# Transformer block in one program: Q and K stacked in two fp32r parts on 32 rows a head instead of six bf16 part products on 64

## The reference, cut to what matters

```python
xn = layernorm(x)
# attention 1: no softmax; causal; weights 1 - tanh^2 of scaled and shifted scores
energy = (where(causal, -10000, q1 @ k1.T * scale) - threshold) / tau
a1 = 1 - tanh(energy)**2;  s = (a1 / (sum(a1) + 1e-6) @ v1) @ Wo.T
# attention 2: plain softmax over all 512 keys, then a mixture of experts
h = rmsnorm(xn);  ctx = softmax(q2 @ k2.T * scale) @ v2;  x1 = xn + ctx @ wo
h2 = rmsnorm(x1); moe = swiglu_shared(h2) + sum over top 2 of 8 experts
out = x + s * silu(x1 + moe)
```

## Time and profile before

| what | us |
|---|---|
| median of 3 runs (1149.69 to 1155.43) | 1154.11 |
| the profiled execution | 1157.05 |
| its span in the trace | 1155.2 |
| first score matmul of row 0 | 76.4 |
| one row of tokens in the middle (from 485.69 to 621.17, L1193 to L1193) | 135.5 |

### The profile page before, as it was taken

How to read it: one execution, slowest core, us unless ns; L and a number is a source line. 1 busy time by engine, 2 the same in 40 slices (tenths; PEclk the granted TensorE clock), 3 DMA queues, 4 the chain that set the end, 5 groups by cost and what they waited for, 6 DMA issues and landing times.

```text
span 1155.2 us, 18598 instructions
## 1 busy us (share of the span) xinstructions
PE 1032.3 (89%) x6912; PEld 471.8 (41%) x6912; DVE 856.3 (74%) x1716; ACT 652.9 (57%) x888; POOL 347.4 (30%) x194
## 2 busy tenths in 40 slices
PE   3459999989999999999999899999999889999998
PEld 1102355324652346423554245522465235542364
DVE  7447687759977597786877589775986869774872
ACT  4027862588326972378624884269723786248831
POOL 6500335103630154303352035400552033520023
PEclk9558999999999999999999999999999999999999
DMA  5540225103441045201251024310342113500020
GB/s 176 117 54 2 49 68 132 34 2 77 109 68 29 3 96 127 38 20 44 64 141 25 11 63 122 69 28 2 96 116 41 30 29 69 148 9 20 1 75 9
DMA packets 71785, 69.65 MB, mean 60 GB/s; under 512 B 8528, under 2 KB 63056, under 8 KB 71568
## 3 DMA queue, kind: packets, MB, share of 16 engines
q1 hardware_dynamic: 68928, 64.41, 24.7%
q10 hardware_dynamic: 2768, 4.06, 1.0%
HBM read 53.37 MB, written 14.81 MB: 59 GB/s over the span
## 4 chain that ended last, share of the span: by engine, by line
PE 56%; DVE 21%; ACT 11%; DMA 4%; issue 3%; SPq 3%; POOL 1%; ACTq 0%; DVEq 0%; POOLq 0%
PE O L1019 9%; PE O L1035 8%; DVE nmax L677 7%; DVE PT L714 7%; ACT PT L554 6%; PE S L1051 6%; PE S L1053 5%; PE S L994 5%; PE S L1052 5%; PE M L963 4%; PE M L960 4%; PE M L946 2%; DVE PT L840 2%; SPq L337 2%; SPq L327 1%
## 5 line engine op out<-in xcount | busy, mean ns | idle before, releaser
L554 ACT ACTIVATE PT<-S 128x1024 f32<-128x1024 f32 (+1 forms) x448 | 420.7, 971 | 117.3 <-PE S L994 115.0
L677 DVE TENSOR_REDUCE nmax<-M 128x1 f32<-128x512 f32 x512 | 330.6, 685 | 119.4 <-PE M L960 80.4
L714 DVE SCALAR_TENSOR_TENSOR PT<-PT 128x768 f32<-128x768 f32 (+1 forms) x192 | 215.6, 1171 | 96.4 <-ACT PT L554 96.0
L1019 PE MATMUL O<-PT,V 128*12 128x256 f32 (+3 forms) x2816 | 242.2, 424 | 0.0
L423 POOL TENSOR_TENSOR split<-split,parts 128x512 f32<-128x512 f32 x32 | 91.0, 2844 | 433.2 <-ACT parts L514 433.2
L438 POOL TENSOR_TENSOR PT<-PT,CB 128x1024 f32<-128x1024 f32 x56 | 133.2, 2385 | 278.0 <-DMA CB<-scrC 158.2
L588 ACT ACTIVATE PT<-S 128x1024 f32<-128x1024 f32 x72 | 73.9, 1027 | 250.7 <-PE S L1053 250.6
L994 PE MATMUL S<-stackQ,stackK 64*128 64x512 bf16 (+3 forms) x1024 | 192.1, 347 | 21.6 <-DMA stackQ<-mTZ 8.4
L1051 PE MATMUL S<-h2hi,wgu_hi 128*128 128x512 f32 x288 | 150.5, 522 | 0.1
L1035 PE MATMUL O<-PT,wdn 128*128 128x512 f32 x288 | 142.7, 595 | 0.0
L960 PE MATMUL M<-KX,stackQ 128*128 128x512 bf16 x256 | 104.3, 409 | 28.5 <-DMA KX<-scrK 21.3
(11 more groups left out here) (189 smaller groups left out, 1042.5 us busy)
## 6 DMA issues: line engine op xcount, KB each, us to landing
CB<-scrC SPq DMA_DIRECT2D x64, 256.0 KB, 5.7
stackQ<-scrQ SPq DMA_DIRECT2D x192, 64.0 KB
stackK<-scrK SPq DMA_DIRECT2D x192, 64.0 KB
scrQ<-parts SPq DMA_DIRECT2D x16, 384.0 KB, 5.0
scrK<-parts SPq DMA_DIRECT2D x16, 384.0 KB, 7.8
KX<-scrK SPq DMA_DIRECT2D x96, 32.0 KB
PT<-in_w_gu ACTq DMA_DIRECT2D x2, 1152.0 KB, 8.0
xin<-in_x SPq DMA_DIRECT2D x8, 256.0 KB, 2.9
```

The source lines that it names most:

```text
L554: a.activation(PT[:, n % SLOTS, 2 * q * w:2 * q * w + 2 * w].rearrange("p (r n) -> p r n", r=2), S[k][:, :].rearrange("p (r n) -> p r n", ...
L677: v.tensor_reduce(nmax[:, h % 2, h // 2, t:t + 1], M[k][:, :], AX.X, ALU.max, negate=True).then_inc(m_read[k], 1)
L714: v.scalar_tensor_tensor(p, p, 1.0, p, ALU.subtract, ALU.mult).then_inc(weighed, 1)
L1019: last = t_.matmul(O[k][32 * q:32 * q + VW, i0:i1], V[:, j, 4 * g + q, :], PT[:, n % SLOTS, w * q + at:w * q + at + i1 - i0], start=(j == ...
```

## The change

`PAIRS` has three products of two parts, (0,0), (0,1) and (1,0), 24 rows a head, and the parts are fp32r in place of bf16. A head takes 32 rows (`SLOT`), the four heads of a group lie above each other, and the row maximum's two parts are rows 24 and 25. `KX` is 128 rows by 4 heads by 2 groups of fp32r. POOL makes the second part in one instruction; the store of a stack is two fp32 parts, its 12 loads are 8 partitions by 4 groups by 512 fp32. The transposes of the maxima take an fp32r identity. The maxima of Y and Z stand directly behind the score pair of a half, those of heads 2 and 3 of a group behind half 0, those of heads 0 and 1 behind half 1.

```diff
-PAIRS = [(0, 0), (0, 1), (0, 2), (1, 0), (1, 1), (2, 0)]
-HP = H // 2
-HALF = 64
+PAIRS = [(0, 0), (0, 1), (1, 0)]
+PARTS = 2
+SLOT = 32
...
-spread(MAX["Y"], {0: 1, 1: 3, 2: 4, 3: 4, 4: 4})
-spread(MAX["Z"], {5: 3, 6: 4, 7: 4, 8: 5})
+spread_beside("Y", {0: (1, 1), 1: (1, 1), 2: (2, 2), 3: (2, 2), 4: (2, 2)})
+spread_beside("Z", {5: (2, 2), 6: (2, 2), 7: (2, 2), 8: (2, 2)})
...
-        parts = [sb(f"parts{i}", [128, 3, L], bf16) for i in range(2)]
-        stack = {n: sb("stack" + n, [128, HP, L], bf16) for n in ("Q2", "K2", "Q1", "K1")}
-        KX = sb("KX", [128, 2, PADDED, L], bf16)
+        parts = [sb(f"parts{i}", [128, PARTS, L], fp32r) for i in range(2)]
+        stack = {n: sb("stack" + n, [128, NG, L], fp32r) for n in ("Q2", "K2", "Q1", "K1")}
+        KX = sb("KX", [128, 4, PADDED, L], fp32r)
...
-                    for r in range(2):
+                    for i in range(4):
                         for c, pair in enumerate(PAIRS):
-                            sp.dma_start(stack[name][HALF * r + HD * c:HALF * r + HD * c + HD, :, :],
-                                         scratch[name][pair[side]].rearrange("(h r d) n -> r d h n", r=2, d=HD)[r])\
+                            sp.dma_start(stack[name][SLOT * i + HD * c:SLOT * i + HD * c + HD, :, :].bitcast(fp32),
+                                         scratch[name][pair[side]].rearrange("(g i d) n -> i d g n", i=4, d=HD)[i])\
...
-                g.tensor_tensor(s[:, :], s[:, :], p[:, 0, :], ALU.subtract).then_inc(pool_step, 1)
-                g.tensor_tensor(p[:, 1, :], s[:, :], ones[:, 0:1].broadcast_to([128, L]), ALU.mult).then_inc(pool_step, 1)
-                g.tensor_tensor(p[:, 2, :], s[:, :], p[:, 1, :], ALU.subtract).then_inc(parts_ready, 1)
+                g.tensor_tensor(parts[i][:, 1, :], split[i][:, :], parts[i][:, 0, :], ALU.subtract).then_inc(parts_ready, 1)
...
-                        rows = slice(HALF * r, HALF * r + HALF)
+                        rows = slice(SLOT * (2 * q + r), SLOT * (2 * q + r) + SLOT)
...
+                    if n < N1:
+                        for q, part in enumerate((names[:u.cut[n]], names[u.cut[n]:])):
+                            scores(it, n, q)
+                            for name in part:
+                                if name[0] == "max":
+                                    work(u, it, name)
+                            if n in v_at and v_at[n] % NT > 0:
+                                with_v(it, v_at[n], q)
+                            elif n in v_at and q == 0:
+                                with_v(it, v_at[n])
+                            for name in part:
+                                if name[0] != "max":
+                                    work(u, it, name)
+                        continue
```

More of the change, by code:

```diff
@@ L51, in width, with blocks, spread, spread_beside @@
     return L if kind == "all" else sum(L - 128 * j for j in js)
-MAX = {run: [("max", 2 * hp + r, t) for hp in range(*pairs) for t in range(NT) for r in range(2)] for run, pairs in RUNS.items()}
+MAX = {run: [] for run in RUNS}
 EXPERT, END = UNITS, UNITS + NE
 PLACES = {n: [] for n in range(END + 1)}
-def spread(work, counts):
-    at = 0
-    for n, count in counts.items():
-        PLACES[n] += work[at:at + count]
-        at += count
-    assert at == len(work)
-spread(MAX["Y"], {0: 1, 1: 3, 2: 4, 3: 4, 4: 4})
-spread(MAX["Z"], {5: 3, 6: 4, 7: 4, 8: 5})
+HALF1 = set()
+def blocks(run, slots):
+    return [("max", 4 * RUNS[run] + i, t) for t in range(NT) for i in slots]
+def spread(run, counts):
+    work = blocks(run, range(4))
+    for n, count in counts.items():
+        PLACES[n] += work[:count]
+        MAX[run] += work[:count]
+        del work[:count]
+    assert not work
+def spread_beside(run, counts):
+    halves = blocks(run, (2, 3)), blocks(run, (0, 1))
+    for n, of_half in counts.items():
+        for half, count in enumerate(of_half):
+            PLACES[n] += halves[half][:count]
+            MAX[run] += halves[half][:count]
+            if half:
+                HALF1.update(halves[half][:count])
+            del halves[half][:count]
+    assert not any(halves)
+spread_beside("Y", {0: (1, 1), 1: (1, 1), 2: (2, 2), 3: (2, 2), 4: (2, 2)})
+spread_beside("Z", {5: (2, 2), 6: (2, 2), 7: (2, 2), 8: (2, 2)})
 PLACES[3].insert(2, "outT")
@@ L105, in __init__ @@
         self.places = {n: [w for w in work if here.get(w, following if w in AHEAD else own)] for n, work in PLACES.items()}
+        self.cut = {n: sum(w not in HALF1 for w in work) if n < N1 else len(work) // 2 for n, work in self.places.items()}
         self.order = [w for n in sorted(self.places) for w in self.places[n]]
@@ L190, in program @@
         ones = sb("ones", [128, 128])
[L191 to L194, removed]
+        identr = sb("identr", [128, 128], fp32r)
+        nmax = sb("nmax", [128, 4, NG, NT])
+        mh = {run: sb("mh" + run, [128, 4 * PARTS * NT], fp32r) for run in RUNS}
+        mT = {run: sb("mT" + run, [4 * PARTS * NT, 128], fp32r) for run in RUNS}
         stats = sb("stats", [128, NT, 6])
@@ L449, in row @@
                 g.tensor_tensor(VS[:, 0, :, :], V1[:, 1, :, 0:HD], VS[:, 1, :, :], ALU.add).then_inc(v_summed, 1)
[L450 to L456, removed]
+                if following:
+                    second_part(u, "Q2")
+                    second_part(u, "K2")
                 for e in range(1, NE - 1):
                     if following and e < 3:
-                        for _step in split_steps(u, ("Q1", "K1")[e - 1], it + 1, True):
-                            pass
+                        second_part(u, ("Q1", "K1")[e - 1])
                     weigh_expert(it, e)
@@ L983, in scores @@
                 key, query = ("K2", "Q2") if n < N1 else ("K1", "Q1")
[L984 removed]
+                at = 0
                 if n >= N1:
@@ L1155, in row @@
                         pe.wait_ge(setup, 2)
-                    for run, (p0, _p1) in RUNS.items():
-                        if n == NT * (p0 // 2) and n:
+                    for run, g in RUNS.items():
+                        if n == NT * g:
                             pe.wait_ge(row_in[run], (it + 1) * 64)
@@ L1187, in row @@
                     work(u, it, "maxT_W")
-                    for q in range(2):
-                        scores(it + 1, 1, q)
-                    for name in ROWS[it + 1].places[0]:
-                        work(ROWS[it + 1], it + 1, name)
+                    second_scores(ROWS[it + 1], it + 1)
                 for t in range(NT):
@@ L1207, in _ @@
             first_scores(0)
-            for q in range(2):
-                scores(0, 1, q)
-            for name in ROWS[0].places[0]:
-                work(ROWS[0], 0, name)
+            second_scores(ROWS[0], 0)
             for it in range(B):
```

111 lines of the change are left out of this document (52 added, 59 removed).

## The result

| | median, us | runs | ratio to before, 95% interval |
|---|---|---|---|
| before | 1154.3 (1149.7 to 1155.4) | 4 | |
| after | 1284.1 (1277.1 to 1293.1) | 4 | 1.114 [1.105, 1.122] |

What follows compares the result with a forecast made beforehand. Bounds: DVE in units 0 to 8, ACT in units 9 to 15, PE in stage 2 and the experts. A row 0 + 0.5 + 0.7 + 0.8 = +2.0, times 8 = +16, start -8: +8, 1162 us; range 1124 to 1194.

Steps and rivals of the forecast that it cites:

- stage 1: Score stage of each row of tokens: no change in units 0 to 8, +0.5 us a row in units 9 to 15.
- units 0 to 8: First half of stage 1, with the maxima of Y and Z: DVE sets the pace, no change, bounds -1.9 and +0.3.
- Units 9 to 15: Second half of stage 1: PE's half units go from 0.87 to 0.97; +0.5 us a row, bounds 0 and +1.4.
- The load: Every score group: the longer fp32r weight load costs PE 0.10 us, bounds 0 and 0.2; pair to product 0.42.
- Stage 2: Per row: loads add 2.9, less a 1.3 wait and 0.9 idle: +0.7 us, bounds -1.3 and +3.5.
- The 1.3 wait: Stage 2, 7 rows: PE's wait for DVE, slowed by POOL's splits, goes with POOL's shorter work: -1.3 us.
- The experts: Expert stretch of each row: slower fp32r maxima and score groups opening twice, +0.8 us, bounds 0 and +1.5.
- Fewer POOL instructions cost nothing here: Experts: POOL's shorter split adds no time, since PE is the bound there.
- The start: Before the first score matmul: earlier stores and larger packets shorten the DMA queue, -8 us, between -3 and -15.
- The loads are not hidden: Against the faster rival: loads hidden at every score group, 0.32 pair to product, 1120 us, chance 0.3.
- They do not queue either: Against the slower rival: neighbouring heads' loads queue, each pair opens 0.2 later, 1214 us, chance 0.12.
- The maxima do run beside the pair: Against the last rival: stage 1 maxima run after the pair, at most +2 a row, 1162 to 1178, chance 0.08.

Runs made afterwards that it cites:

- runs with fillers: Kernel after, with 2, 4 or 8 overwritten bf16 full-array matmuls ahead of each stage 1 score pair: 1261.5 to 1330.5, 1237.1 and 1273.3 us.
- fp32r run with 64 rows: Kernel after, stage 1 scores and maxima of Y and Z contracting over 64 rows at a time, Exp's scale lowered: 1194.2 us (one run).
- the order alone: Kernel before (bf16, 64 rows a head) with only the change's new places of the maxima: 1160.3 us, ratio 1.005.
- run with POOL's part alone: Kernel before with one POOL instruction a tensor making the second bf16 part, third part left out: 1149.9 us, ratio 0.996.
- run with four fillers: Kernel after, with four overwritten bf16 matmuls of 128 x 128 and 128 columns ahead of each stage 1 score pair: 1237.1 us, ratio 1.070.
- run with the start alone: Kernel before with only the maxima rows of X and W sent ahead of K1's loads at the start: 1150.1 us, ratio 0.996.
- run with POOL's late weighing: Kernel before, one POOL instruction a tensor, but three for the following row's Q1 and K1, delaying the second expert's weighing; third part unused: 1140.3 us, ratio 0.985.
- eight fillers: Kernel after, with eight overwritten bf16 matmuls of 128 x 128 and 128 columns ahead of each stage 1 score pair: 1273.3 us, ratio 1.102.

## Why the prediction was wrong, step by step

**The step that failed is stage 1**, "I take no change, bounds -1.9 and +0.3" and "+0.5, bounds 0 and +1.4". Its prices came from rows at clock 1.00, and the sum had no term for what the change does to the clock: the clock was taken as unchanged without a reason. The measured change is +115.2 in 8 rows, 14.4 a row, of which by the runs with fillers and with 64 rows some 11 is the clock and some 3.5 the change itself at full clock (an estimate). The trace of before could have warned: in the earlier trace rows two maxima on `KX` take 1.01 us, where 0.22 + 0.39 = 0.61 would do by the earlier trace rows; the page's clock row has a 5 in its second and third slice; and from 76.4 to 92.9 stage 1 runs at 0.50 with PE at work. That the array's filling is the cause could not be read from it; it has no stretch of 32-row matmuls.

**At full clock units 0 to 8 were mis-sized too.** In the fp32r run with 64 rows, stage 1 is +3.3 against +0.5. Units 9 to 15 are as forecast, half units of 394.72 - 393.74 = 0.98 for 0.97, and from unit 9's first pair to the end 15.3 for 14.4, inside the bounds of 0 and +1.4. The other 2.4 lie in units 0 to 8, where I took DVE's pace to hide the loads and the order to cost nothing; the order alone cost 0.7 there in bf16. In that run the maxima do not run beside the pair, so how much of the rest holds for the change itself stays open. The bound of -1.9 does not come out of its own terms either: 22.3 - 23.9 is -1.6, and DVE's idle time is 2.2.

```profile
393.74 0.50 PE L997 MATMUL S<-stackQ,stackK 64*128 64x512 f32 x2
394.17 0.62 PE L1022 MATMUL O<-PT,V 128*12 128x256 f32 x8
394.72 0.50 PE L997 MATMUL S<-stackQ,stackK 64*128 64x512 f32 x2
```

**The load was right.** 0.42 from pair to product was forecast, 0.43 measured at full clock; PE's busy time in stage 2 grew by 37.57 - 34.87 = 2.70, forecast 2.9.

**Stage 2 was right**, +0.4 or +0.5 in six of the 8 rows for +0.7 forecast (+0.9 as a mean, with the half clock in the fourth row and +1.9 in the last). The 1.3 wait of the transposes of OS for DVE is gone, as a run with POOL's part alone confirms: -1.5.

**The experts** took +1.0 to +1.5 in the first seven rows for +0.8 forecast, inside the bounds of 0 and +1.5, but not for the reasons given alone. "Fewer POOL instructions cost nothing here" was wrong: the run with POOL's part alone is 0.8 to 1.3 longer there.

**The start** was right in its direction, -11.0 for -8, though that is one profile against one: in the run with four fillers, which is the same up to there, `KX` landed at 40.9, 4.6 later than here. The queue did stop being last: `KX` landed at 36.3 instead of 42.25, the rows of X went out at 54.75, and the first score stands directly behind the transpose of W.

```profile
54.75 2.74 SPq L356 DMA_DIRECT2D stackQ<-mTX  x4
```

```profile
65.13 0.31 PE L972 MATMUL M<-identr,mhW 128*32 128x128 f32 x1 [1.28 <-DVE mhW L690]
65.38 0.80 PE L997 MATMUL S<-stackQ,stackK 32*128 32x512 f32 x4
```

**The rivals.** The loads are not hidden (0.43). They do not queue either (0.5 and more was its mark). The maxima do run beside the pair. None of the rivals named the clock; the slower one's 1214 came nearest to the time by a mechanism that is not there.

## What to carry to other kernels

A change that narrows what matmuls fill of the array is to be priced twice, once at each level of the clock, before anything else is counted; read the granted clock of every stretch of the kernel before and ask which stretches the change makes like the slow ones. When a wait is removed, follow the engine that is now early: POOL's second expert, weighed sooner, took back most of what POOL's shorter split had won.

## What the runs showed of the hardware

- The granted clock fell from 1.00 to 0.50, and stayed there with PE busy 47.01 of 47.80 us, in matmuls on 32 rows of fp32r (stage 1 of the kernel after); in bf16 on 32 rows it did the same (33.33 of 34.20). In stage 1 of rows 2 to 8 it stayed at 1.00 with 64 rows of fp32r, and with four matmuls of 128 x 128 added to each pair. What brings it back 3 us before the end of stage 1 no run isolates.
- Pairs on 64 rows do not keep 1.00 always: in bf16 they ran from 76.4 to 92.9 at 0.50 at the start of the kernel before, and two of the runs with them have one short fall in a stage 1 (from 513.50 in the run with the start alone, from 510.57 in the run with POOL's late weighing).
- Stage 2 after also has 32-row pairs and keeps 1.00 in most rows; there masks and projections of 128 rows stand between them. That this is why was not tested. In the runs with 64 rows of fp32r and with eight fillers it has one short fall each (from 1131.47 and from 618.10).
- Matmuls on different rows of the array start together: pair and maxima at 393.75 and 393.76.
- A DVE instruction of 0.29 took 1.78 beside one of POOL, six times as long, against 1.75 and 1.6 times for the larger ones of the earlier trace rows.
